# Routed experts in tiles of 384 and 256 rows, with their outputs in a scratch of their own

## The reference

```python
z = _layernorm(h)                                          # 2976 rows of H = 256
probs = softmax(z @ router_w)                              # E_ROUTED = 8 experts
top_k_prob, top_k_idx = jax.lax.top_k(probs, 2)            # two experts per row
_expert = lambda z, up, down: gelu(z @ up) @ down          # 256 -> F = 1024 -> 256
h = h + z + _expert(z, shared_up[0], shared_down[0]) \
      + sum(gates[..., e:e+1] * _expert(z, routed_up[e], routed_down[e]) for e in range(8))
```

## Time and profile before

| | |
|---|---|
| median of 3 runs | 1132.03 us (1131.85 to 1132.82) |
| the profiled execution | 1133.0 us |
| its span in the trace | 1131.4 us |
| PE busy | 1054.6 us, 93% |
| DVE, ACT, POOL busy | 610.4, 524.3, 419.8 us |
| moved by DMA | 99.01 MB, mean 88 GB/s |
| granted TensorE clock, mean | 0.98 |

### The profile page before, as it was taken

How to read it: one execution, slowest core, us unless ns; L and a number is a source line. 1 busy time by engine, 2 the same in 40 slices (tenths; PEclk the granted TensorE clock), 3 DMA queues, 4 the chain that set the end, 5 groups by cost and what they waited for, 6 DMA issues and landing times. The chain is left out here.

```text
span 1131.4 us, 25575 instructions
## 1 busy us (share of the span) xinstructions
PE 1054.6 (93%) x8756; PEld 977.4 (86%) x8757; DVE 610.4 (54%) x1660; ACT 524.3 (46%) x1277; POOL 419.8 (37%) x505
## 2 busy tenths in 40 slices
PE   5994999999999999999998899999999999998998
PEld 5993888888788888888887799999999999998898
DVE  3664666767686776767767653323323323423464
ACT  3542545444544444444444454445444544544252
POOL 2000232344352524334252325153646065063882
PEclk9996999999999999999998899999999999999999
DMA  9517990001000100000011414313331321311653
GB/s 189 123 35 241 353 346 28 29 20 37 15 14 27 27 27 23 31 14 14 31 26 55 156 55 140 121 42 116 118 114 46 121 98 60 113 45 43 163 144 104
DMA packets 81568, 99.01 MB, mean 88 GB/s; under 512 B 29968, under 2 KB 64496, under 8 KB 81520
## 3 DMA queue, kind: packets, MB, share of 16 engines
q1 hardware_dynamic: 57648, 58.87, 17.2%
q0 software_dynamic: 18176, 29.12, 8.8%
q10 hardware_dynamic: 5696, 10.39, 2.6%
HBM read 50.48 MB, written 47.74 MB: 87 GB/s over the span
## 5 line engine op out<-in xcount | busy, mean ns | idle before, releaser
L1218 POOL TENSOR_TENSOR prob<-prob,rc 93x372 f32<-93x372 f32 x128 | 102.9, 804 | 317.5 <-DVE rc L1113 316.9
L852 PE MATMUL pj_ps<-xg,wA 128*128 128x372 f32 x768 | 154.3, 348 | 7.8 <-DVE xg L696 5.0
L1701 DVE TENSOR_TENSOR act_s<-dn_ps,act_s 128x256 fp32r<-128x256 f32 x112 | 47.6, 425 | 205.5 <-ACT act_s L1580 205.5
L852 PEld LDWEIGHTS pj_ps<-xg,wA 128*128 128x128 f32 x768 | 130.2, 191 | 18.0 <-DVE xg L696 4.9
L840 PE MATMUL pj_ps<-wB,xg 128*93 128x512 f32 x384 | 102.6, 403 | 0.0
L1009 ACT ACTIVATE probT<-t_ps 93x372 f32<-93x372 f32 x128 | 60.6, 474 | 89.6 <-PE t_ps L873 88.3
L1476 PE MATMUL up_ps<-rx,wB 128*128 128x256 f32 x720 | 89.1, 281 | 4.5 <-ACT act_s L1580 2.8
L1476 PEld LDWEIGHTS up_ps<-rx,wB 128*128 128x128 f32 x720 | 85.6, 188 | 6.9 <-ACT act_s L1580 3.6
L1117 DVE TENSOR_TENSOR oT<-o_ps,oT 128x372 fp32r<-128x372 f32 x64 | 34.8, 543 | 105.2 <-ACT oT L1014 104.1
L1490 PE MATMUL dn_ps<-wB,act_s 128*128 128x256 f32 x720 | 88.3, 282 | 0.0
L1490 PEld LDWEIGHTS dn_ps<-wB,act_s 128*128 128x128 f32 x720 | 85.7, 188 | 0.0
(11 more groups left out here) (175 smaller groups left out, 2078.8 us busy)
## 6 DMA issues: line engine op xcount, KB each, us to landing
slots<-zeros SPq DMA_DIRECT2D x8, 3072.0 KB, 23.5
rows_in<-slots SPq DMA_DIRECT2D x29, 256.0 KB, 2.6
raw<-in_L_ffn_routed_up POOLq DMA_DIRECT2D x7, 1024.0 KB, 5.4
raw<-in_L_ffn_routed_down POOLq DMA_DIRECT2D x7, 1024.0 KB, 8.4
slots<-rows_out ACTq DMA_DIRECT2D x28, 256.0 KB, 2.0
ln_out<-split SPq DMA_DIRECT2D x8, 744.0 KB
frames<-in_x SPq DMA_DIRECT2D x8, 400.0 KB
raw_w<-in_L_attn_kernel SPq DMA_DIRECT2D x6, 512.0 KB, 5.6
```

The costliest lines, as they stand in the source:

```text
L852: ins = pe.matmul(pj_ps[:, t, 0:N], wA[:, wp, at:at + P], xg[:, dp, m, :], start=(k == 0), stop=(k == 5))
L1218: pool.tensor_tensor(p, p, rc[:, u % 2, :].unsqueeze(2).broadcast_to([TP, 4, SL]), ALU.mult).then_inc(scaled, 1)
L1701: dve.tensor_tensor(act_s[:, LO, f, 0:ET], act_ps[f % 2], act_s[:, HI, f, 0:ET], ALU.subtract).then_inc(ract_lo, 1)
```

## The change

The routed experts now take tiles of 384 rows (`WIDE`) and of 256 rows (`NARROW`): every expert has at least one of each, and with 7 chunks of 128 rows or more the two counts add up to the rows rounded up to 128. With the rows given above the wide tiles are 2, 1, 1, 2, 1, 1, 2, 1 (11) and the narrow ones 2, 1, 1, 1, 2, 1, 1, 1 (10). Each tile, wide or narrow, loads, transposes and splits 384 rows, and copies and stores 384 rows of output; only the matmuls, gelus and subtractions go by its width. `count_tiles` works on all 124 partitions with two tables that POOL writes at the start of attention, and also packs the three numbers of an expert into one, which PE loads and takes apart; ACT, DVE and SP load three numbers.

The second gelu is written in place over its bank of `up_ps`, behind the rounded one, with a semaphore between; the bank is free once DVE has subtracted (`ract_lo`). The copy of `dn_ps` to `rows_out` has moved from ACT to DVE, between the subtractions of blocks 1 and 2 of the next tile (`put_y`), and ACT issues its store behind the gelus of block 4 (`store_y`). The outputs go to a new scratch, `y_rows`, 384 rows per tile, which SP fills with zeros (five transfers of 2688 rows) behind the zeros of `slots`. Since an output no longer lies at its input's place, DVE works out where each lies (`find_places`) ahead of the last expert's loop.

```diff
-    ET = 256
-    MAXT = -(-B * SL // ET)
-    CAP = MAXT * ET
+    WIDE, NARROW = 3 * P, 2 * P
+    MAXK = -(-B * SL // P)
+    CAP = MAXK * P
+    MAXB, MAXA = MAXK // 3, 3
+    TT = 2 * E + (2 * B * SL // P + E) // 3
...
+    slots = nc.dram_tensor("slots", (E * CAP + P, HD), F32).ap()
+    y_rows = nc.dram_tensor("y_rows", ((TT + 1) * WIDE, HD), F32).ap()
...
+                sp.dma_start(slots[E * CAP:E * CAP + P, :], zeros[:, 0:HD].bitcast(F32)).then_inc(cleared, 16)
+                for i in range(5):
+                    part = (TT + 1) * WIDE // 5
+                    sp.dma_start(y_rows[i * part:(i + 1) * part, :].rearrange("(a p) n -> p a n", p=P),
+                                 zeros[:, 0:HD].bitcast(F32).unsqueeze(1).broadcast_to([P, part // P, HD])).then_inc(y_cleared, 16)
...
+            def tiles_in_one(eng, e):
+
+                v = eng.value_load(tiles_i[0:1, 3, bass.ds(e, 1)], min_val=5, max_val=64 * TT + 63)
+                wide = eng.snap(((v >> 2) & 15).with_bounds(min_val=1, max_val=MAXB))
+                narrow = eng.snap((v & 3).with_bounds(min_val=1, max_val=MAXA))
+                return wide, narrow, eng.snap((v >> 6).with_bounds(min_val=0, max_val=TT))
...
+                def load_rows(n0, row):
+                    sp.wait_ge(xt_done, 1 + n0)
+                    sp.dma_start(rows_in[:, :, :], slots[bass.ds(row, WIDE), :].rearrange("(a p) n -> p a n", p=P)
+                                 ).then_inc(rows_loaded, 16)
...
-                        for a in range(2):
-                            ins = pe.transpose(tr_ps[:, 0, (2 * m + a) * P:(2 * m + a + 1) * P],
-                                               rows_in[:, a, m * P:(m + 1) * P], ident[:, :])
+                        for a in range(3):
+                            ins = pe.transpose(tr_ps[:, m, a * P:(a + 1) * P], rows_in[:, a, m * P:(m + 1) * P], ident[:, :])
...
-                        pe.wait_ge(rgelu_done, 1 + n0 * FC + max(f - 3, 0))
+                        pe.wait_ge(ract_lo, 1 + n0 * FC + max(f - 3, 0))
...
+                        wide, narrow, t0 = tiles_in_one(pe, e)
+                        with pe.Fori(0, wide) as t:
+                            tile(weights[par], e, t0 + t, WIDE)
+                        with pe.Fori(0, narrow) as t:
+                            tile(weights[par], e, t0 + wide + t, NARROW)
...
+                def store_y(n0):
+                    act.wait_ge(y_out, 1 + n0)
+                    act.dma_start(y_rows[bass.ds(y_row(n0), WIDE), :].rearrange("(a p) n -> p a n", p=P), rows_out[:, :, :]
+                                  ).then_inc(y_stored, 16)
+
+                def tile(n0, width):
+                    for f in range(FC):
+                        act.wait_ge(rup_done, n0 * FC + (f + 1))
+                        if f == 0:
+                            act.wait_ge(rdn_done, 1 + n0)
+                        act.activation(act_s[:, HI, f, 0:width], up_ps[:, f % 4, 0:width], ACT.Gelu).then_inc(ract_hi, 1)
+                        act.wait_ge(ract_hi, n0 * FC + (f + 1))
+                        act.activation(up_ps[:, f % 4, 0:width], up_ps[:, f % 4, 0:width], ACT.Gelu).then_inc(rgelu_done, 1)
+                        if f == 4:
+                            store_y(n0)
+                    take_x(n0 + 1)
+
                 with act.Fori(0, E) as e:
-                    n, t0 = tiles_of(act, e)
-                    with act.Fori(0, n) as t:
-                        n0 = t0 + t
-                        for f in range(FC):
-                            act.wait_ge(rup_done, n0 * FC + (f + 1))
-                            act.wait_ge(ract_lo, 1 + n0 * FC + max(f - 1, 0))
-                            act.activation(act_ps[f % 2], up_ps[:, f % 4, 0:ET], ACT.Gelu)
-                            if f == 0:
-                                act.wait_ge(rdn_done, 1 + n0)
-                            act.activation(act_s[:, HI, f, 0:ET], up_ps[:, f % 4, 0:ET], ACT.Gelu).then_inc(rgelu_done, 1)
-                        take_x(n0 + 1)
-                        act.wait_ge(rdn_done, 1 + n0 + 1)
-                        act.wait_ge(y_stored, 1 + n0 * 16)
-                        act.activation(rows_out[:, :, :].rearrange("p a n -> p (a n)"), dn_ps[:, 0, :], ACT.Copy
-                                       ).then_inc(y_out, 1)
-                        act.wait_ge(y_out, 1 + n0 + 1)
-                        act.dma_start(slots[bass.ds(first_row(e, t), ET), :].rearrange("(p a) n -> p a n", a=2),
-                                      rows_out[:, :, :]).then_inc(y_stored, 16)
...
+                def find_places():
+
+                    ch = Chain(dve, m_chain)
+                    at = slot_q[:, :, :].rearrange("p k c -> p (k c)")
+                    all_edges, all_jumps = (t[:, :, :].rearrange("p i e -> p (i e)") for t in (edges, jumps))
+                    wide = [R, 2 * NC, 3 * E]
+                    for i in (1, 2):
+                        ins = dve.tensor_scalar(edges[:, i, :], tiles_f[:, 0, :], float(WIDE), float(i * NARROW), ALU.mult, ALU.add)
+                    dve.tensor_scalar(jumps[:, 0, 1:E], found[:, 0:E - 1], float(WIDE), float(-CAP - 2 * P), ALU.mult, ALU.add)
+                    dve.memset(jumps[:, 0, 0:1], float(WIDE))
+                    ch.then(dve.memset(jumps[:, 1:3, :], float(P)))
+                    ch.then(dve.tensor_scalar(edges[:, 1:3, :], edges[:, 1:3, :], float(CAP), None, ALU.min))
+                    ch.then(dve.tensor_tensor(edges[:, 1:3, :], edges[:, 1:3, :],
+                                              edges[:, 0:1, :].broadcast_to([R, 2, E]), ALU.add))
+                    ch.then(dve.tensor_tensor(beyond[:, :, :], at.unsqueeze(2).broadcast_to(wide),
+                                              all_edges.unsqueeze(1).broadcast_to(wide), ALU.is_ge))
+                    ch.then(dve.tensor_tensor(beyond[:, :, :], beyond[:, :, :], all_jumps.unsqueeze(1).broadcast_to(wide), ALU.mult))
+                    ch.then(dve.tensor_reduce(moved[:, :], beyond[:, :, :], AX, ALU.add))
+                    dve.tensor_tensor(y_at[:, :, :].rearrange("p k c -> p (k c)"), moved[:, :], at, ALU.add).then_inc(y_at_set, 1)
...
+                def put_y(n0):
+                    dve.wait_ge(rdn_done, 1 + n0)
+                    dve.wait_ge(y_stored, 1 + n0 * 16)
+                    dve.tensor_copy(rows_out[:, :, :].rearrange("p a n -> p (a n)"),
+                                    dn_ps[:, :, :].rearrange("p b n -> p (b n)")[:, 0:3 * HD]).then_inc(y_out, 1)
+
+                def tile(n0, width):
+                    for f in range(FC):
+                        dve.wait_ge(rgelu_done, 1 + n0 * FC + (f + 1))
+                        dve.tensor_tensor(act_s[:, LO, f, 0:width], up_ps[:, f % 4, 0:width], act_s[:, HI, f, 0:width],
+                                          ALU.subtract).then_inc(ract_lo, 1)
+                        if f == 1:
+                            put_y(n0)
+                    take_x(n0 + 1)
...
+                with dve.Fori(0, E - 1) as e:
+                    expert(e)
+                find_places()
+                put_y(expert(E - 1))
```

More of the change, by code:

```diff
@@ L1374, in _ @@
                         pool.indirect_dma_start(
-                            out=y_ring(b, k), out_offset=None, in_=slots,
-                            in_offset=bass.IndirectOffsetOnAxis(ap=slot_q[:, k, b:b + 1], axis=0)
+                            out=y_ring(b, k), out_offset=None, in_=y_rows,
+                            in_offset=bass.IndirectOffsetOnAxis(ap=y_at[:, k, b:b + 1], axis=0)
                             ).then_inc(gathered[b % YR], 16)
@@ L1482, in tile @@
                     pe.wait_ge(summed, G1 * C)
-                    for a in range(2):
+                    for a in range(width // P):
                         k = 0
@@ L1509, in _ @@
                 pe.wait_ge(taken[0], number(LG, "logits"))
+                pe.wait_ge(taken[1], number(LG, "rank"))
                 turn_rows(0)
@@ L1517, in _ @@
                         e = i * 2 + par
[L1518 to L1520 removed]
+                        wide, narrow, t0 = tiles_in_one(pe, e)
[3 more added lines that the diff above has]
+                            tile(weights[par], e, t0 + wide + t, NARROW)
                 pe.wait_ge(w_split, E + 1)
[L1523 to L1525 removed]
+                wide, narrow, t0 = tiles_of(pe, E - 1)
+                pe.wait_ge(x_lo, t0 + wide + narrow + 1)
                 up(wB, G1)
+                pe.wait_ge(y_out, 1 + t0 + wide + narrow)
                 down(wB, G1)
@@ L1590, in _ @@
+                with act.Fori(0, E) as e:
+                    wide, narrow, t0 = tiles_of(act, e)
+                    with act.Fori(0, wide) as t:
+                        tile(t0 + t, WIDE)
+                    with act.Fori(0, narrow) as t:
+                        tile(t0 + wide + t, NARROW)
+                wide, narrow, t0 = tiles_of(act, E - 1)
+                store_y(t0 + wide + narrow)
                 gelus(G1)
```

(21 more changed lines are left out.)

142 lines of the change are left out of this document (82 added, 60 removed).

## The result

The changed kernel takes 1101.14 us (median, 1099.94 to 1101.4) against 1132.03 before: a ratio of 0.9717, 95% interval 0.9701 to 0.9733. It is faster, as forecast, but the forecast was 1108.0 with a range from 1103.5: the gain is 30.9 us where 24.3 were worked out. The profiled execution has a span of 1098.9 us.

A forecast was written before the change was run, and what follows sets the result against it. PE, busy for 93% of the span, was taken as the bound. Stage 315.3 against 342.3 us (-27.0), ahead +1.9, behind +0.8 gave -24.3 from 1133.0; with the median 1.0 lower, forecast 1108 us, range 1103.5 to 1114.

The forecast's parts named there:

- The down chunk: Routed stage, down matmuls: 24 matmuls per chunk of 128 rows, priced at 2.82 us, for 53 chunks.
- The wide up: Up matmuls of a wide tile: 48 of 384 columns take 8.45 us, between 8.19 and 8.54.
- Narrow tiles: Routed tiles of 256 rows: up 5.69, transposes 0.66, down 5.64, together 11.99 us; 10 of them 119.9.
- The even count at block 6: Narrow tiles: block 2 subtracted at 4.25 us, bank wanted at 4.27; 0.5 us allowed in all, bounds 0 and 4.
- Borders: Seven borders between experts: ACT no longer waits for the last down, so 12.2 us go; 0.3 left for all seven.
- find_places: DVE ahead of the last expert: 5.4 us of work stalls PE 1.0 us at block 4, bounds 0 and 3.
- First tile: Ahead of the first routed tile: counting, loads, transposes and splits add 1.9 us, bounds +0.5 and +4.
- Behind: Behind the last routed tile: slower copy (+0.35) and store (+0.4) ahead of the gathers add 0.8 us, bounds 0 and 3.
- rival 1: Routed tiles: PE waits for DVE in every tile, 0.8 us narrow and 0.3 wide, 11 us: 1119; chance 0.12.
- rival 2: Routed loops on PE: returns in the longer loop wait for instruction fetches, 16 us: 1124; chance 0.04.
- rival 3: Routed stage: the change saves no rows, every expert rounding up as before to 56 chunks: 1125; chance 0.03.
- rival 4: Output copy in put_y holds the banks: no gain from a 2.6 us copy on, 1137 at 3 us; chance 0.03.

The follow-up runs named there:

- Experiments 2: The changed kernel with the rows of act_s 388 elements apart instead of 384: 1105.81 us.
- 3: The changed kernel with routed down matmuls loading 124 instead of 128 columns of act_s at the same offsets: 1107.15 us.
- Experiments 1: The kernel before with the rows of act_s 384 elements apart instead of 372, nothing else: 1131.85 us, ratio 0.9998.
- Experiment 4: The changed kernel's scheme with all tiles of 256 rows, 28 of them: 1126.07 us, ratio 0.9939 to the kernel before.
- experiment 6: The changed kernel with the output copy behind block 3 instead of 1 and the store behind block 6 instead of 4: 1101.79 us.

## Why the prediction was right in kind and short in size

- **The down chunk (the step that failed).** It was priced at 5.64 / 2 = 2.82 us, as if the matmul's pace were the instruction's own, and without a bound. It is 8.19 / 3 or 5.46 / 2 = 2.73 in 16 of 21 tiles. With 8.18 ten times, 8.48 once, 5.46 six times and 5.66 four times, the downs take 145.7 us, not 53 x 2.82 = 149.5: -3.8. Experiments 2 and 3 show that the fast pace goes when `act_s` has rows 388 apart or 124 columns are loaded; the change made `act_s` wider and got the pace beside. Experiments 1 and 4 show that the pitch of 384 isn't enough: 5 of 28 and 1 of 28 downs are fast there. No bound in the prediction covered this term, and without it the time would have been some 1105, inside the range.
- **The wide up.** 8.32 in a steady tile, where 8.45 was taken from a slope to the price of 372 columns. The starts of those wander (0.163 to 0.173 in the up at 1031.8), 384 run evenly at 0.1733; why isn't tested, and these ups don't read `act_s`. Three at 8.36 to 8.41, each the first behind a return of PE's outer loop, and the first at 8.77 (0.3 was allowed for it) leave -1.1, inside the stated bounds.
- **Narrow tiles.** The even count at block 6 was a gate: in 8 of 10 tiles the starts there are 0.17 us further apart, more than the 0.1 that the prediction named as a sign of being wrong, and experiment 6 prices gate and slower pace behind it at 0.22 us. But the 5.69 taken for the up already held a like wait of the kernel before (at block 4, with the slower pace behind it), so that the 0.5 was charged twice; with 5.66 to 5.69 measured it is -0.7.
- **Borders.** 12.2 us were said to go, and went; 0.3 was left and nothing was paid: -0.3. Experiment 4 shows the stage of 28 tiles at 331.7 against 342.3 (with 1.2 us paid ahead of the last expert, for `find_places`). That one load on PE would be free and three not (+10.6) was not seen: the prediction had -0.3 for it ahead of the first tile only.
- **`find_places`.** Forecast 1.0 of waiting. It began at 965.34 and its last step at 970.30; DVE's first subtraction behind it came at 972.41. The profile gives PE 0.17 us of idle time there, but its starts at block 4 are 0.33 and 0.11 further apart than elsewhere, so the price is 0.4: -0.6.
- **First tile.** Forecast +1.9. Counted from the start of the shared expert's second up it is 37.0 us against 35.4, +1.6. Attention itself ended 1 us sooner in this execution, so that only +0.6 is seen. In the profiles with the changed kernel's code up to there the first routed matmul stands between 687.9 and 691.6, so that 1 us is chance.
- **Behind.** +0.4 for +0.8; copy 0.97 and store 2.56, near the 0.95 and 2.4 worked out. The sixth gather landed 4.57 us after its issue.

The terms of the stage add up to -6.5, which is the 6.5 us by which it (308.8) fell short of 315.3. With the first tile (-1.3) and the part behind (-0.4) the two profiled executions lie 8.2 us further apart than worked out; the medians, 30.9 us apart, missed by 6.6. The first tile's share of that is luck.

The rivals: beside the last expert's 0.4, PE loses no more than 0.2 us to DVE in a tile (rival 1). Queue 8, which has 31 instruction packets in all against 29 before, carries five of them from 681 to 777 us and none from 777 to 1019 (queue 14 has one, at 966.5), while PE goes round both loops, so the longer loop is not fetched again, as the trace of attention's loop had suggested and against the two-page rule of the Trainium skill ("Runtime: NRT & Kernel Launch", Instruction fetch mechanics) quoted there; the same section gives PE's instruction memory room for 2048 instructions, and with that the trace agrees (rival 2). 2406 instructions of PE in the stage are 53 chunks (rival 3). The copy takes 0.95 and not 2.6 us (rival 4; its sum for a copy of 3 us, 10 x 2.05 + 11 x 1.15, gives 1141 and not 1137, which changes nothing here).

The range was too narrow on the low side. All prices came from one kernel's pace, and none of the stage's terms came out longer than priced: the starts of the matmuls of 372 and of 256 columns wandered in the kernel before, and a wait lay in the price of the narrow up. A mean pace between the 0.1133 and 0.118 that single stretches of the trace of before show should have been read as two paces, with the lower as a bound.

## What to carry to other kernels

Before pricing a matmul from a mean, look at its single starts: where they wander, or take one of two values, the mean is not a price that another layout or order must keep, and the lower value is the bound. Count the loads of registers on the bound engine: at the end of a dynamic loop one was hidden here where three cost 1 us. Before gaining a microsecond in a stage, look at what the next stage does with an idle PE: a wait that leaves PE still, here for 5 us, is paid twice, once as the wait and once at 1.2 GHz. And before reading a microsecond of a tail from one profile, look at how far that tail differs in another profile of the same code: here by 1.6 (100.8 against 102.4).

## What the runs showed of the hardware

- Matmuls of 256 columns started every 0.1133 or 0.1177 us at the full clock, regularly and for a whole down but its first few, with the stationary operand 128 wide and its rows 384 elements apart; with rows 372 or 388 apart or 124 columns their starts varied between 0.112 and 0.125, at 0.1175 to 0.1184 on average. No other pitch was tried, and what picks one of the two paces is open.
- An up of 256 columns that followed its down without a gap started in the down's pace, 197 of 197 times. Behind a wide up, 10 of 11 downs were fast with 6 transposes between, behind a narrow one 6 of 10; with 8 transposes all were.
- After a wait inside an up of 256 columns PE went on at 0.1177, where it had run at 0.1133 (kernel before, up at 724.3: the first 24 starts 0.113 to 0.115 apart, all 22 behind the wait at block 4 from 0.117 to 0.121; with the copy later and no wait, up at 735.6: all 47 gaps 0.113 to 0.115).
- With three loads of registers on PE at a border the starts around it were 0.94 to 1.43 us apart, with one 0.11 to 0.12.
- A PE loop of some 990 instructions went round with no instruction packet on queue 8 from 777 to 1019 us; the first gap behind a return of the outer loop was 0.04 to 0.09 us longer than elsewhere.
- Behind a stand of 5 us (1006 to 1011) PE ran at a granted clock of 0.51 for the next 6.2. A second such fall stood in the tails of some profiles and not of others, also with the same code there (the kernel with 8 transposes against the changed one).
